# One-hots of an edge's target, kept in DRAM by two walks and loaded by seven

## The reference

```python
x = layernorm(x + transformer(x))      # 4 heads: softmax over each target's edges of q[dst].k[src], sum of p*v[src]
x = layernorm(x + relational(x))       # 86 relation types, 16 bases, tanh gate on (x_hat . y_hat)
x = layernorm(x + smoothing(x))        # three times X = segment_sum(w * X[col], row)
x = layernorm(x + attention(x))        # three GATv2 layers, 8 heads x 32, each with a batch normalisation
```

## Time and profile before

| what | value |
|---|---|
| median of 3 runs | 10508.26 us (10503.42 to 10534.5) |
| the profiled execution's own time | 10509.52 us |
| its span | 10507.6 us |
| TensorE busy (matmul, weight load) | 7619.7 us (73%), 5671.4 us (54%) |
| VectorE busy | 7188.9 us (68%) |
| ScalarE busy | 1582.9 us (15%) |
| GpSimd busy | 5226.6 us (50%) |
| moved by DMA | 947.03 MB, 90 GB/s over the span |

### The profile page before, as it was taken

The page is one execution under the profiler, slowest core; times in us unless marked ns, Lnnn a source line. Parts: engine busy times, 40 slices in busy tenths (PEclk is TensorE's granted clock), DMA queues, the critical chain, the costliest instruction groups (busy, mean ns, idle before and its releaser), DMA issues. The chain is left out here.

```text
span 10507.6 us, 173882 instructions
## 1 busy us (share of the span) xinstructions
PE 7619.7 (73%) x34427; PEld 5671.4 (54%) x34428; DVE 7188.9 (68%) x12981; ACT 1582.9 (15%) x4852; POOL 5226.6 (50%) x6235
## 2 busy tenths in 40 slices
PE   0888859899997777656666559766664986666398
PEld 0788859788875444324444346544443664444266
DVE  2233346699965777405888779788877978887698
ACT  0222211233320000001111011211111121111011
POOL 1677730377754888503777500277770007777100
PEclk9999999899998999867999789799987979999698
DMA  5333351122231333573555631255573115555510
GB/s 23 52 60 61 60 53 40 35 46 46 46 32 56 110 110 110 201 289 111 137 137 137 111 72 31 59 137 137 137 125 76 37 33 137 137 137 134 93 37 23
DMA packets 1413037, 947.03 MB, mean 90 GB/s; under 512 B 916254, under 2 KB 1276695, under 8 KB 1412434
## 3 DMA queue, kind: packets, MB, share of 16 engines
q0 software_dynamic: 184960, 458.42, 20.2%
q1 hardware_dynamic: 1131794, 427.96, 17.2%
q10 hardware_dynamic: 96192, 59.54, 1.8%
HBM read 697.23 MB, written 248.11 MB: 90 GB/s over the span
## 5 line engine op out<-in xcount | busy, mean ns | idle before, releaser
L845 PE MATMUL ps<-rows,ohT 128*128 x7040 | 2178.6, 450 | 1346.1 <-DMA gx<-table_g,gi 668.2
L629 POOL DMA_INDIRECT gx<-table_g,gi x2640 | 2503.1, 948 | 802.6 <-issue 726.2
L845 PEld LDWEIGHTS ps<-rows,ohT 128*128 128x128 f32 x7040 | 1448.0, 248 | 1915.0 <-DMA gx<-table_g,gi 976.9
L1134 PE MATMUL ps<-work,oh 128*128 128x273 f32 (+1 forms) x7040 | 1778.9, 408 | 345.0 <-DVE oh L648 336.9
L1134 PEld LDWEIGHTS ps<-work,oh 128*128 128x128 f32 x7040 | 1340.7, 228 | 782.2 <-issue 434.9
L614 POOL COPY gi<-src_i 128x16 int32 (+1 forms) x280 | 57.6, 206 | 2466.4 <-POOLq L508 2404.2
L734 DVE TENSOR_TENSOR work<-gx,ps 128x768 f32<-128x768 f32 x660 | 629.8, 954 | 732.5 <-PE ps L847 731.7
L1099 DVE TENSOR_TENSOR work<-rows,xl 128x1024 f32<-128x1024 f32 (+1 forms) x880 | 871.6, 991 | 319.1 <-DMA xl<-xs_g 146.6
L795 ACT CAST ohT<-ps 128x512 f32<-128x512 bf16 x888 | 520.2, 586 | 3639.9 <-PE ps L828 3622.2
L629 POOL DMA_INDIRECT gx<-table_r,gi x880 | 833.0, 947 | 269.9 <-issue 207.4
L629 POOL DMA_INDIRECT gx<-table_t,gi x880 | 832.7, 946 | 264.7 <-issue 209.9
(11 more groups left out here) (307 smaller groups left out, 9331.6 us busy)
## 6 DMA issues: line engine op xcount, KB each, us to landing
big<-dense_d SPq DMA_DIRECT2D x96, 784.0 KB
dense_d<-big SPq DMA_DIRECT2D x588, 98.0 KB
dense_d<-big ACTq DMA_DIRECT2D x588, 98.0 KB
gx<-table_g,gi POOLq DMA_INDIRECT x2640
xs_g<-gx SPq DMA_DIRECT2D x660, 64.0 KB
xl<-xs_g SPq DMA_DIRECT2D x660, 64.0 KB, 1.8
rows<-dense_d SPq DMA_DIRECT2D x48, 784.0 KB
type_d<-work SPq DMA_DIRECT2D x220, 96.0 KB
```

The source lines that it names most:

```text
L629: pool.indirect_dma_start(m.gx[:, u, k, 0:w], None, table, bass.IndirectOffsetOnAxis(m.gi[:, odd, u * K + k:u * K + k + 1].bitcast(U32), 0 ...
L845: ins = nc.tensor.matmul(to, turned, rows, start=True, stop=not adds)
L1134: ins = nc.tensor.matmul(sums(u), m.oh[:, u, k, :], rhs(u % 2)[:, k, :], start=(k == 0), stop=(k == K - 1))
```

## The change

Two DRAM arrays of 220 groups x 128 x 512 fp32 are added, 256 KB for a group: `hot_d` for the one-hots, `hotT_d` for the transposes. The walks of "t" still make both matrices. In the `logits` walk of "t", SP stores each group's `ohT` (`keep_hot`), and ScalarE's next copy into the same half waits for that store (`kept`). In `weighted_sums` of "t", ScalarE's queue stores each group's one-hot, and VectorE's `one_hot` four groups later waits for it.

The seven later walks load instead of making: `logits` of g0 to g2 loads the transposes into the four-deep `oh` ring (`load_hot`, two groups ahead); `weighted_sums` of g0 to g2 loads the one-hots next to `xl`; `relation_walk` loads the one-hots (four-deep) and the transposes (two-deep). In them the one-hot instructions on VectorE, the transposes on TensorE and the copies on ScalarE are gone. The diff, cut to its core:

```diff
+    m.hot_d = dram("hot_d", [G, P, K * P])
+    m.hotT_d = dram("hotT_d", [G, P, K * P])
...
@@ logits, vector
-                need(dve, s("turned"), g)
-                one_hot(nc, m, g + 3, (u + 3) % RING, True, node_no).then_inc(s("one_hot"), 1)
                 if not gat:
+                    need(dve, s("turned"), g)
+                    one_hot(nc, m, g + 3, (u + 3) % RING, True, node_no).then_inc(s("one_hot"), 1)
...
@@ logits, scalar
-            def turn(g, half):
+            def turn(g, half, kept):
                 act.wait_ge(s("turned"), g + 1)
                 need(act, s("projected"), g - 1)
+                need(act, s(f"kept{half}"), kept)
                 nc.scalar.copy(m.ohT[:, half, :], turned_b(half)).then_inc(s("ohT"), 1)
...
-                turn(i * RING + u + 2, u % 2)
-                if not gat:
-                    type_turn(i * RING + u, u % 2)
-                    if u:
-                        type_out(i, u - 1)
-                    elif not isinstance(i, int) or i:
-                        type_out(i - 1, RING - 1)
-            for g in range(2):
-                turn(g, g)
-            groups(act, body)
+                turn(i * RING + u + 2, u % 2, 16 * (i * (RING // 2) + u // 2 + 1))
+                type_turn(i * RING + u, u % 2)
+                if u:
+                    type_out(i, u - 1)
+                elif not isinstance(i, int) or i:
+                    type_out(i - 1, RING - 1)
+            if not gat:
+                for g in range(2):
+                    turn(g, g, 0)
+                groups(act, body)
...
@@ logits, tensor
-                pe.wait_ge(s("ohT"), g + 1)
+                if gat:
+                    pe.wait_ge(s(f"hotT{slot}"), 16 * turns_done)
+                else:
+                    pe.wait_ge(s("ohT"), g + 1)
...
-                    to, turned = m.psA[:, half, k * cols:(k + 1) * cols], m.ohT[:, half, k * P:(k + 1) * P]
+                    to = m.psA[:, half, k * cols:(k + 1) * cols]
+                    turned = m.oh[:, slot, k, :] if gat else m.ohT[:, half, k * P:(k + 1) * P]
...
@@ logits, sync
+            def load_hot(g, slot):
+                need(sp, s("projected"), g - RING + 1)
+                sp.dma_start(m.oh[:, slot, :, :].rearrange("p k q -> p (k q)"),
+                             m.hotT_d[bass.ds(g, 1)].rearrange("a p w -> (a p) w")).then_inc(s(f"hotT{slot}"), 16)
+
+            def keep_hot(g, half):
+                sp.wait_ge(s("ohT"), g + 1)
+                sp.dma_start(m.hotT_d[bass.ds(g, 1)].rearrange("a p w -> (a p) w"), m.ohT[:, half, :]
+                             ).then_inc(s(f"kept{half}"), 16)
+
             def body(i, u):
                 g = i * RING + u
+                if not gat:
+                    keep_hot(g, u % 2)
+                elif not isinstance(i, int) or i < G // RING - 1 or u < RING - 2:
+                    load_hot(g + 2, (u + 2) % RING)
                 sp.wait_ge(s(f"rows{u}"), 16 * K * (i + 1))
...
@@ weighted_sums, sync
+                if gat:
+                    sp.dma_start(m.oh[:, u, :, :].rearrange("p k q -> p (k q)"),
+                                 m.hot_d[bass.ds(g, 1)].rearrange("a p w -> (a p) w")).then_inc(s(f"hot{u}"), 16)
...
@@ weighted_sums, vector
-                one_hot(nc, m, g, u).then_inc(s("one_hot"), 1)
+                if not gat:
+                    need(dve, s(f"kept{u}"), 16 * i)
+                    one_hot(nc, m, g, u).then_inc(s("one_hot"), 1)
...
@@ weighted_sums, scalar
+                    act.wait_ge(s("one_hot"), g + 1)
+                    act.dma_start(m.hot_d[bass.ds(g, 1)].rearrange("a p w -> (a p) w"),
+                                  m.oh[:, u, :, :].rearrange("p k q -> p (k q)")).then_inc(s(f"kept{u}"), 16)
             in_parts(act, body)
+            for u in range(0 if gat else RING):
+                act.wait_ge(s(f"kept{u}"), 16 * turns)
...
@@ weighted_sums, tensor
-                pe.wait_ge(s("one_hot"), g + 1)
+                if gat:
+                    pe.wait_ge(s(f"hot{u}"), 16 * (i + 1))
+                else:
+                    pe.wait_ge(s("one_hot"), g + 1)
...
@@ relation_walk, sync
+                need(sp, s("added"), g - RING + 1)
+                sp.dma_start(m.oh[:, u, :, :].rearrange("p k q -> p (k q)"),
+                             m.hot_d[bass.ds(g, 1)].rearrange("a p w -> (a p) w")).then_inc(s(f"hot{u}"), 16)
+                need(sp, s("fetched"), g - 1)
+                sp.dma_start(m.ohT[:, u % 2, :], m.hotT_d[bass.ds(g, 1)].rearrange("a p w -> (a p) w")
+                             ).then_inc(s(f"hotT{u % 2}"), 16)
...
@@ relation_walk, vector
-                    node_hot(g + 3, (u + 3) % RING)
                     scaled(g + 1, (u + 1) % RING)
...
@@ relation_walk, scalar
-                narrow(g + 2, (u + 2) % RING)
-                turn(g + 2, u % 2)
...
@@ relation_walk, tensor
-            def add(g, slot):
+            def add(g, slot, turns_done):
                 half = slot % 2
+                pe.wait_ge(s(f"hot{slot}"), 16 * turns_done)
...
-                pe.wait_ge(s("ohT"), g + 1)
+                pe.wait_ge(s(f"hotT{half}"), 16 * loads)
...
-            def body(i, u):
+            def body(i, u, last=False):
                 g = i * RING + u
-                fetch(g + 1, (u + 1) % 2)
-                turn(g + 2, (u + 2) % RING)
-                add(g, u)
-            for g in range(2):
-                turn(g, g)
-            fetch(0, 0)
-            groups(pe, body)
+                if not last:
+                    fetch(g + 1, (u + 1) % 2, i * (RING // 2) + (u + 1) // 2 + 1)
+                add(g, u, i + 1)
+            fetch(0, 0, 1)
+            groups(pe, body, G // RING - 1)
+            for u in range(RING):
+                body(G // RING - 1, u, last=u == RING - 1)
```

More of the change, by code:

```diff
@@ L136, in allocate @@
     m.type_in = rows[:, at:at + RING * K * TYPE_W].rearrange("p (n k w) -> p n k w", n=RING, k=K)
-    at += RING * K * TYPE_W
-    m.node_b = rows[:, at:at + K * P].bitcast(BF16).rearrange("p (n k q) -> p n k q", n=2, k=K)
     m.big = sb("big", [P, 2 * RUN * H3])
@@ L686, in logits @@
     att_row = m.psC[:, 0, 0:W3] if gat else None
-    node_no = m.psC[:, 0, W3:W3 + P] if gat else m.psA[:, 0, 512:512 + P]
+    node_no = m.psA[:, 0, 512:512 + P]
     def type_turned():
@@ L776, in _ @@
             if gat:
-                nc.vector.tensor_copy(att_row, m.att3[:, layer, :])
-            nc.vector.tensor_copy(node_no, m.iota_row[:, :]).then_inc(s("rows_set"), 1)
+                nc.vector.tensor_copy(att_row, m.att3[:, layer, :]).then_inc(s("rows_set"), 1)
+            else:
+                nc.vector.tensor_copy(node_no, m.iota_row[:, :]).then_inc(s("rows_set"), 1)
             dve.wait_ge(s("rows_set"), 1)
-            for g in range(3):
+            for g in range(0 if gat else 3):
                 one_hot(nc, m, g, g, True, node_no).then_inc(s("one_hot"), 1)
@@ L870, in body @@
                     project(g + 1, (u + 1) % RING, i + 1 if u < RING - 1 else i + 2)
-                turn(g + 2, (u + 2) % RING)
                 if not gat:
+                    turn(g + 2, (u + 2) % RING)
                     type_turn(g, u % 2)
@@ L875, in body @@
                         type_rows(g - 1, (u + 1) % 2)
-            for g in range(2):
+            for g in range(0 if gat else 2):
                 turn(g, g)
@@ L912, in body @@
                     store_types(g - 1, (u + 1) % 2)
-            groups(sp, body)
+            if gat:
+                for g in range(2):
+                    load_hot(g, g)
+            groups(sp, body, G // RING - 1)
+            for u in range(RING):
+                body(G // RING - 1, u)
             if not gat:
@@ L921, in _ @@
                 sp.wait_ge(s(f"type_stored{half}"), 16 * (G // 2))
+                sp.wait_ge(s(f"kept{half}"), 16 * (G // 2))
 def softmax_parts(nc, m, name, heads):
@@ L1221, in _ @@
         def _(dve):
-            def node_hot(g, slot):
-                one_hot(nc, m, g, slot, False, node_no).then_inc(s("node_hot"), 1)
             def collect(g, half, blk=None):
@@ L1296, in _ @@
         def _(act):
[L1297 to L1305, removed]
             def tanh(g, half):
@@ L1315, in body @@
                 g = i * RING + u
-                narrow(g + 2, (u + 2) % RING)
-                turn(g + 2, u % 2)
                 if not last:
                     tanh(g + 1, (u + 1) % 2)
-            for g in range(2):
-                narrow(g, g)
-                turn(g, g)
             tanh(0, 0)
@@ L1329, in _ @@
         def _(pe):
[L1330 to L1334, removed]
-                                              m.ident_b[:, :])
-                ins.then_inc(s("turned"), 1)
-            def add(g, slot):
+            def add(g, slot, turns_done):
                 half = slot % 2
+                pe.wait_ge(s(f"hot{slot}"), 16 * turns_done)
                 pe.wait_ge(s("rhs"), g + 1)
@@ L1348, in add, with fetch @@
```

(4 more changed lines are left out.)

3 lines of the change are left out of this document (1 added, 2 removed).

## The result

The changed kernel takes 10380.05 us (median of 4 runs, 10375.68 to 10392.64), against 10510.47 us (4 runs, 10503.42 to 10534.5) for the kernel before beside it: ratio 0.9874, 95% interval 0.9856 to 0.9892. It is 130 us faster, 37 less than the 167 forecast, and lies in the range of 10280 to 10440. The profiled execution took 10392.64 us, with a span of 10390.7.

The account below looks back on a forecast made before the run. GpSimd's issue was taken to bound five gathering walks, TensorE the transformer's weighted sums, VectorE and TensorE by turns attention's. Terms -173 - 5 + 3 + 8 = -167 us gave 10341 us, range 10280 to 10440.

Parts of the forecast that it names:

- Attention's weighted sums, -173: Three walks without the one-hot instruction: period from 2.19 to 1.90 us a group, 58 us saved a walk, 173 in three.
- The three candidates: Attention's weighted sums, possible periods per group: VectorE 1.70 us, TensorE 1.88, loop through two right-hand sides 1.90; largest taken.
- the gapless 4.18 us of the earlier trace: Attention's weighted sums: 16 TensorE records, 2.09 us a group; basis of the rival that TensorE already bounds, 10466 us, chance 0.09.
- Transformer's weighted sums, +8: One walk storing one-hots: TensorE stays the bound; 8 us added for the final wait and later `xl` loads, bounds 2 and 25.
- Five gathering walks set by GpSimd's issue: Logits and relation walks: four indirect DMAs take 4.99 us a group, so less work on VectorE won't shorten them.
- Attention's logits, "Saved: 0": Three walks: removed work lies beside GpSimd's 4.99 us, and the 256 KB load, asked 10 us ahead, lands in about 2.5.
- transformer's logits, "+3 us for the last landing": First walk: the store per group is hidden at 2.5 us landing; 3 us added, bounds 0 and 240 us.
- the 3.0 us of the store loop: Transformer's logits: store, landing and ScalarE's next copies must fit into 4.99 us, costing nothing up to 3.0 us of landing.
- The rival with the stores: Transformer's logits: store loop becomes the bound, up to 10581 us; chance 0.06 for landings of 3.0 to 3.7 us, 0.04 beyond.
- signs of being wrong: Profile after: L1134 waiting for one-hots' DMA; L795 waiting for `hotT_d`, first walk above 1150 us; GpSimd idle longer for DMA.
- Relation walk, -5: Relation walk: GpSimd's real waits for VectorE are about 8 us; a lighter VectorE gives back 5, bounds 0 and 8.
- the rival of GpSimd's waits: Gathering walks: added loads slow the gathers; each 0.2 us in 880 groups costs 176 us and cancels the gain; chance 0.04.

Follow-up runs that it names:

- others_only: The changed kernel, except that attention's weighted sums make their one-hots as before; 10568.75 us, 1.0037 of the kernel before.
- double: The changed kernel with another 256 KB loaded per group in attention's weighted sums; 10442.56 us, 0.9917 of the kernel before.
- rhs4: The changed kernel with four right-hand side buffers instead of two in the weighted sums; 10372.41 us, 0.9851 of the kernel before.
- again: The changed kernel run a second time without edit; 10388.34 us, 0.9866 of the kernel before.
- before_spread: The kernel before with the padding edges' source numbers spread over the nodes; 10366.88 us, 0.9852 of the kernel before.
- best: The kernel before with one-hots stored and loaded for attention's weighted sums only, padding sources spread and four right-hand side buffers; 10166.31 us, 0.9653.
- best_again: The kernel before with one-hots loaded in attention's weighted sums only, padding spread, four right-hand sides, run once more; 10172.75 us, 0.9668.
- sums_only: The kernel before with one-hots stored by the transformer's weighted sums and loaded only by attention's; 10362.24 us, 0.984 of the kernel before.
- spread: The changed kernel with the padding edges' source numbers spread over the nodes; 10212.48 us, 0.9696 of the kernel before.

## Why the prediction was right, and by what it was off

- *Attention's weighted sums, -173*: the executions give -174, `others_only` by its ratio 180. The three candidates were weighed rightly: TensorE isn't the bound at 2.09 (the period is 1.89), the loads aren't late (`double` shows how much more it takes), and the loop through two right-hand sides is, as `rhs4` shows by taking it away. That the gapless 4.18 us of the earlier trace rows was no pace of TensorE's came out of the weight loads beside it.
- *Transformer's weighted sums, +8*: 5.5.
- *Five gathering walks set by GpSimd's issue*: right. An indirect DMA still takes 0.944 to 0.947 us, with 851 us less on VectorE. The granted clock over g0's logits fell from 0.89 to 0.81, without a loss to the body, as worked out.
- *Attention's logits, "Saved: 0"; transformer's logits, "+3 us for the last landing"*: these are the terms that were mis-sized, at +19 and +14 (+28 and +16 in `again`). The step that failed is the landing time. I took one value, 2.5 us with bounds of 2.3 and 4.1, for the whole walk. In the body it was good (2.1 to 3.1). In the tail it is 9.9 us for the loads, and the stores keep L797 waiting up to 13.0; against that neither two groups' advance nor the 3.0 us of the store loop holds. The rival with the stores had its place and its mechanism right, and I priced it only as all or nothing over 220 groups. The sign was in the rows: the earlier trace rows gave 4.99 us a group and 1097 us for a walk that took 1139, and I left those 42 us unread. 29 of them were the tail, as `before_spread` shows, where the DMA share is 0.90 at 45 GB/s.
- Two of the signs of being wrong that the prediction named were there, inside a total that held: L795 (now L797) of the transformer waits for `hotT_d`, with a first walk of 1153.4 us, above the 1150; and GpSimd waits longer for a DMA, the store of `xs_g`. The transformer's walk also isn't within 10 us of its length. They point at the same failed step.
- *Relation walk, -5*: the whole stage has +3 in this execution and -3 in `again`, and can't tell, as the 86 to 121 us behind its last gather differ by 14 between `best` and `best_again`, the same kernel (85.7 and 99.7). The gathers can: the 209th group's first gather starts 1052.2 us behind the walk's first before and 1044.9 after; in `sums_only` and `spread`, the executions with the longer gather, it is 1052.8 and 1047.7. So the walk's body gave back 5 to 7 us, and the tail took most of it again. GpSimd's one wait of 5.8 us was most of it; after the change, over the same walk:

```profile
POOL gx L629 <- DVE work L1304: 22.7, 72, 1.1
```

- Of the medians' 37 us less gain, the 30 of the logits walks and the 8 of the relation walk, less 2 and 1 for the sums, make 35. That is a sum over one execution, without the dense matrices' 17, and the interval of the ratio is 0.18%, 19 us, to either side.
- That the loads jam the *gathers* themselves, the rival of GpSimd's waits, didn't show in the body, though the share in g0's logits is 0.74 there.

## What to carry to other kernels

A price taken from a steady stretch holds for that stretch. When 220 x (the period) falls 42 us short of the walk, look at the windows of its ends before adding a transfer, and price the transfer's landing where the DMA engines are busiest, which needn't be where they move most. Dropping an instruction that ends a wait is worth the distance to the next loop: write down every candidate (engines and loops through buffers), as the largest is the new period. Padding that points all gathers to one row costs as much as a good optimisation brings: here 1.5% for three lines.

## What the runs showed of the hardware

- Gathers that read one DRAM row again and again: 0.725 us a packet in the mean, against 0.081 with various rows and 0.093 with the padding spread. About half of the queue's packets carry 4 bytes; those of 2 KB alone (eight rows of 256 B) took 1.45 us against 0.15. They also delay DMAs of other queues: 256 KB landed in 9.9 us instead of 3.0.
- The same GpSimd instruction (128 x 196, fp32) had a mean of 771 to 775 ns in nine executions and 784 in three, which makes 17 us of a stage of 1077. The median of the transformer's gathers was 944 to 947 ns, which makes up to 2.6 us of each gathering walk.
- The DMA engines moved 299 GB/s at a share of 0.92, mostly in 2 KB rows; the transfer that was late for its reader was the small one (64 KB, landing in 3.5 us instead of 1.9).
